# A graph network with expert layers: signals for four groups together, and selections made eight groups ahead, in three of its four edge sums

## The reference

```python
def _gcn_layer(x, W, b, src, dst, norm, n_nodes):      # layers 0 and 1
    xt = x @ W
    msg = xt[src] * norm[:, None]
    agg = jax.ops.segment_sum(msg, dst, num_segments=n_nodes)
    return jax.nn.relu(agg + b)

def gcn_conv(h, W, b):                                 # layers 2 and 3
    m = (h @ W)[src] * norm[:, None]
    return jax.ops.segment_sum(m, dst, num_segments=n) + b

x = x + _L0_gnn_ref(_layernorm(x), ...)                # edge sums 0 and 1
x = x + _L0_ffn_ref(_layernorm(x)[None], ...)[0]       # two of eight experts for all nodes
x = x + _L1_gnn_ref(_layernorm(x), ...)                # edge sums 2 and 3
x = x + _L1_ffn_ref(_layernorm(x)[None], ...)[0]       # one of eight experts for each node
```

## Time and profile before

| what | value |
|---|---|
| device time, median of 3 | 6543.07 us (6539.58 to 6545.11) |
| the profiled execution | 6551.94 us, span 6550.3 us |
| busy, share of the span | PE 55%, PE's weight loads 41%, DVE 39%, ACT 14%, POOL 54% |
| layer 0, layer 1 | gathers from 233 and 1701 us on |
| layer 2, layer 3 | gathers from 3420 and 4687 us on |
| gathers | 3328, 946 ns each |
| mean granted clock of TensorE | 0.755 |

### The profile page before, as it was taken

The page is one execution under the profiler, slowest core; times in us unless marked ns, Lnnn a source line. Parts: engine busy times, 40 slices in busy tenths (PEclk is TensorE's granted clock), DMA queues, the critical chain, the costliest instruction groups (busy, mean ns, idle before and its releaser), DMA issues.

```text
span 6550.3 us, 48736 instructions
## 1 busy us (share of the span) xinstructions
PE 3613.2 (55%) x14645; PEld 2676.9 (41%) x14646; DVE 2556.9 (39%) x6904; ACT 934.1 (14%) x2571; POOL 3523.5 (54%) x3846
## 2 busy tenths in 40 slices
PE   7475444444644434358984444444644444457899
PEld 6353333333433323245663332333433333346566
DVE  7366545555343334335442322222322222233244
ACT  6303222222200000012220000000200000004221
POOL 7705666666466666640006666666366666652232
PEclk9788766767876766678996676676767777676999
DMA  2403333333333333320013333333333333323321
GB/s 82 130 3 107 92 90 93 91 92 88 101 92 91 92 92 92 89 63 20 17 34 91 92 94 91 92 92 92 92 88 92 95 89 92 92 83 124 91 94 47
DMA packets 281242, 552.98 MB, mean 84 GB/s; under 512 B 86322, under 2 KB 167075, under 8 KB 280977
## 3 DMA queue, kind: packets, MB, share of 16 engines
q0 software_dynamic: 168496, 457.67, 24.5%
q1 hardware_dynamic: 106214, 85.77, 4.2%
q10 hardware_dynamic: 6268, 6.40, 0.3%
HBM read 490.90 MB, written 61.69 MB: 84 GB/s over the span
## 4 chain that ended last, share of the span: by engine, by line
another core or an unknown queue 37%; PE 29%; DVE 16%; issue 10%; ACT 3%; POOL 2%; DVEq 2%; DMA 1%; SPq 0%; ACTq 0%; POOLq 0%
PE PSA L740 10%; DVE ACC L1475 5%; PE PSA L983 3%; PE PSA L973 3%; PE PSA L863 3%; PE PSA L875 3%; DVE XIN L1448 2%; POOL WORK L565 2%; DVE XIN L1622 1%; DVE XT L1448 1%; PE PSA L694 1%; PE PSA L700 1%; PE PSA L786 1%; ACT ACC L1019 1%
## 5 line engine op out<-in xcount | busy, mean ns | idle before, releaser
L565 POOL DMA_INDIRECT WORK<-tab,SRC x3284 | 3106.6, 946 | 2424.0 <-issue 992.6
L740 PE MATMUL PSA<-WORK,XIN 128*128 128x256 f32 x3984 | 1300.9, 491 | 1543.2 <-DVE XIN L1448 507.0
L1475 DVE TENSOR_TENSOR ACC<-ACC,PSA 64x256 f32 x1664 | 696.2, 418 | 2982.2 <-remote 2361.6
L740 PEld LDWEIGHTS PSA<-WORK,XIN 128*128 128x128 f32 x3984 | 959.7, 249 | 1875.3 <-issue 1522.7
L740 PE MATMUL PSA<-WORK,XT 128*128 128x256 f32 x2584 | 845.8, 490 | 1058.2 <-DVE XT L1448 342.5
L740 PEld LDWEIGHTS PSA<-WORK,XT 128*128 128x128 f32 x2584 | 621.2, 249 | 1271.3 <-issue 1055.6
L1059 ACT ACTIVATE WORK<-PSA 128x256 f32<-128x256 f32 x147 | 54.0, 376 | 2462.3 <-PE PSA L773 2461.9
L1448 DVE TENSOR_TENSOR XIN<-PSA,DST 128x512 f32<-128x512 f32 x378 | 256.3, 679 | 1.9 <-DVE PSA L1459 1.7
L983 PE MATMUL PSA<-ACC,WORK 128*128 128x256 f32 (+1 forms) x1024 | 223.2, 380 | 6.1 <-ACT WORK L1249 6.1
L973 PE MATMUL PSA<-WORK,ACC 128*128 128x489 f32 (+1 forms) x512 | 214.3, 579 | 5.1 <-ACT WORK L1239 5.1
L983 PEld LDWEIGHTS PSA<-ACC,WORK 128*128 128x128 f32 (+1 forms) x1024 | 189.0, 185 | 43.0 <-ACT WORK L1249 12.4
(11 more groups left out here) (282 smaller groups left out, 3478.2 us busy)
## 6 DMA issues: line engine op xcount, KB each, us to landing
WORK<-tab,SRC POOLq DMA_INDIRECT x3284
ACC<-in_L_ffn_w SPq DMA_DIRECT2D x16, 1024.0 KB
tab<-WORK SPq DMA_DIRECT2D x98, 128.0 KB, 1.7
tab<-ACC SPq DMA_DIRECT2D x98, 128.0 KB, 1.8
slots_x<-FILL SPq DMA_DIRECT2D x4, 2080.0 KB
ACC<-slots_x SPq DMA_DIRECT2D x8, 910.0 KB
before_y<-X SPq DMA_DIRECT2D x7, 896.0 KB
X<-in_x ACTq DMA_DIRECT2D x1, 6144.0 KB
```

What stands on the lines that cost most here:

```text
L565: po.indirect_dma_start(out=rows[:, 0:width], out_offset=None, in_=tab[:, :], in_offset=bass.IndirectOffsetOnAxis(ap=SRC[:, c:c + 1].bitca ...
L740: last = pe.matmul(PS[h][:, 0:D], chosen[:, j * P:(j + 1) * P], rows[:, 0:D], start=(j == 0), stop=(j == Q - 1))
L1475: return ve.tensor_tensor(rows, rows, PS[h][half, 0:D], ALU.add)
```

## The change

In layers 1 to 3 the groups are put in batches (`starts`): 51 of four groups and, at the end, one of two and two of one. PE raises `s_p` only with the last matmul of a batch, by the number of groups in it, and DVE waits only ahead of a batch's first add, for the whole batch. The sums of a batch go to one pair of banks, two groups in a bank (`sums_of`); batches take the pairs `PS[0]`, `PS[1]` and `PS[2]`, `PS[3]` in turn, and PE waits at `s_free`, ahead of the first group that it writes to a bank, until the groups that stood there two batches before are added (`last_in_bank`). Adds still raise `s_free` for each group. Selections are made `FAR` = 8 groups ahead, in eight buffers of their own, `SELF`, in `WORK` behind the ring of rows. Layer 0 keeps its order; its calls only name the bank in another way.

```diff
+FAR = 8
...
+        SELF = [WORK[:, RS_ * Q * ROW1 + k * Q * P:RS_ * Q * ROW1 + (k + 1) * Q * P] for k in range(FAR)]
...
+        starts = list(range(0, NGR - 4, 4)) + [NGR - 4, NGR - 2, NGR - 1, NGR]
+
+        def batch_of(layer, g):
+
+            if not layer:
+                return g, g + 1
+            k = max(k for k in range(len(starts)) if starts[k] <= g)
+            return starts[k], starts[k + 1]
+
+        def sums_of(layer, g):
+
+            if not layer:
+                return PS[g % 4][:, 0:D]
+            k = max(k for k in range(len(starts)) if starts[k] <= g)
+            pos = g - starts[k]
+            return PS[k % 2 * 2 + pos // 2][:, pos % 2 * D:(pos % 2 + 1) * D]
+
+        def last_in_bank(layer, g):
+
+            k = max(k for k in range(len(starts)) if starts[k] <= g)
+            pos = g - starts[k]
+            if not layer or pos % 2 or k < 2:
+                return None
+            return min(starts[k - 2] + pos + 1, starts[k - 1] - 1)
+
+        def chosen_of(layer, g):
+            return SELF[g % FAR] if layer else SEL[g % NS]
...
-                    product(SEL[g % NS], rows_of(layer, g), g % 4).then_inc(s_p, 1)
+                    if last_in_bank(layer, g) is not None:
+                        pe.wait_ge(s_free, 4 + NGR * layer + last_in_bank(layer, g) + 1)
+                    last = product(chosen_of(layer, g), rows_of(layer, g), sums_of(layer, g))
+                    first, end = batch_of(layer, g)
+                    if g == end - 1:
+                        last.then_inc(s_p, end - first)
...
                         for j in range(Q):
                             c = Q * g + j
-                            last = ve.tensor_scalar(SEL[g % NS][:, j * P:(j + 1) * P], PLACES, DST[:, c:c + 1],
+                            last = ve.tensor_scalar(SELF[g % FAR][:, j * P:(j + 1) * P], PLACES, DST[:, c:c + 1],
                                                     NRM[:, c:c + 1], ALU.is_equal, ALU.mult)
                         last.then_inc(s_sel, 1)
                     else:
-                        place(SEL[g % NS], edges(DST, g)).then_inc(s_sel, 1)
+                        place(SELF[g % FAR], edges(DST, g)).then_inc(s_sel, 1)
...
-                for g in range(AHEAD):
+                for g in range(FAR):
                     load_spots(g)
                     choose(g)
 
                 for g in range(NGR):
                     spot = spots_of(g)
-                    ve.wait_ge(s_p, NGR * layer + g + 1)
-                    add_sums(g % 4, spot).then_inc(s_free, 1)
-                    if g + AHEAD < NGR:
-                        load_spots(g + AHEAD)
-                        choose(g + AHEAD)
+                    first, end = batch_of(layer, g)
+                    if g == first:
+                        ve.wait_ge(s_p, NGR * layer + end)
+                    add_sums(sums_of(layer, g), spot).then_inc(s_free, 1)
+                    if g + FAR < NGR:
+                        load_spots(g + FAR)
+                        choose(g + FAR)
                     between(g)
                     ve.wait_ge(s_free, 4 + NGR * layer + g + 1)
```

More of the change, by code:

```diff
@@ L736, in _, with product @@
             pe.reg_mov(turn, 16 * Q)
-            def product(chosen, tiles, h):
+            def product(chosen, tiles, into):
                 for j, rows in enumerate(tiles):
-                    last = pe.matmul(PS[h][:, 0:D], chosen[:, j * P:(j + 1) * P], rows[:, 0:D],
+                    last = pe.matmul(into, chosen[:, j * P:(j + 1) * P], rows[:, 0:D],
                                      start=(j == 0), stop=(j == Q - 1))
@@ L762, in sum_edges @@
                                 pe.wait_ge(s_mx, pe.snap(more))
-                                product(SELX, ROWS[0:Q], 0).then_inc(s_pe, 1)
+                                product(SELX, ROWS[0:Q], PS[0][:, 0:D]).then_inc(s_pe, 1)
                                 pe.reg_add(more, more, 1)
@@ L1469, in sum_of, with add_half, add_sums @@
                 return ve.tensor_reduce(into, by_window(weighted), AX.X, ALU.add)
-            def add_half(h, upper, spot):
+            def add_half(sums, upper, spot):
                 half = slice(P // 2, P) if upper else slice(0, P // 2)
                 rows = ACC[half, bass.ds(spot, D)]
-                return ve.tensor_tensor(rows, rows, PS[h][half, 0:D], ALU.add)
-            def add_sums(h, spot):
-                add_half(h, True, spot[0])
-                return add_half(h, False, spot[1])
+                return ve.tensor_tensor(rows, rows, sums[half, :], ALU.add)
+            def add_sums(sums, spot):
+                add_half(sums, True, spot[0])
+                return add_half(sums, False, spot[1])
             def a_tile(v):
@@ L1519, in wide_groups @@
                                 ve.reg_add(zu, zu, D)
-                                chained(add_half(0, True, a_tile(ve.snap(zl))))
-                                chained(add_half(0, False, a_tile(ve.snap(zu))))
+                                chained(add_half(PS[0][:, 0:D], True, a_tile(ve.snap(zl))))
+                                chained(add_half(PS[0][:, 0:D], False, a_tile(ve.snap(zu))))
                                 ve.reg_mov(zx_next, zl)
@@ L1607, in sum_weighted @@
                     ve.wait_ge(s_p, g + 1)
-                    step(add_sums(g % 4, spot))
+                    step(add_sums(sums_of(0, g), spot))
                     settle()
```

## The result

The changed kernel takes 6555.67 us (20 runs, 6543.0 to 6562.34) against 6543.76 us for the kernel before, run beside it (20 runs, 6538.71 to 6554.74): a ratio of 1.0016, with an interval of 1.0009 to 1.0022. The forecast was 6160 us with a range of 6080 to 6510; the time lies outside it, on the side of no gain. The profiled execution took 6557.08 us (span 6555.4).

The account below looks back on a forecast made before the run. POOL's gathers, stopped by late PE signals, were taken as the bound: 6551.94 us less 457.1 (438.4 surplus, 18.7 tail) gives 6094.8; 75 us of remaining pauses makes 6170, with the 0.14% about 6160, range 6080 to 6510.

Parts of the forecast that it names:

- What bounds the kernel now: Layers 1 to 3: POOL's gathers wait for DVE's adds, which wait for PE's queued signals; surplus 438.4 us.
- What remains: Layers 1 to 3: signals 20 us apart mostly drain; 5 pauses a layer of 5 us stay, 75 us.
- Signals: PE to DVE: 54 signals a layer in place of 208, 20.0 us apart in place of 5.0.
- Selections eight ahead: DVE's selections: PE's 419.3 us of waits in layer 1 go, but by itself this moves nothing POOL waits for.
- What the batch costs: Batch's first sum told 15 us later; free if signals are less than 13.3 us late, before 28.3.
- New waits: PE's waits for adds before reusing a bank pair, and about 100 wait instructions: zero cost.
- The tail: Layer ends, last gather to last add: 6.7 us in place of 15.3, 13.4 and 10.1, saving 18.7 us.
- The floor: Layers 1 to 3 if POOL never stops, 1038.8 us of gathers each: 457.1 us off, 6094.8 us.
- B: Rival: lateness grows with gathers since POOL last stood; 26 stops a layer, 6504 up to 6552 us; chance 0.13.
- A: Rival: lateness grows with signal count, only POOL's pause clears it; 13 pauses a layer, 6290 us; chance 0.27.
- C: Rival: signals pass only in POOL's pause, one pause per batch; 51 a layer, 6878 us; chance 0.08.
- D: Rival: the matmul itself is late, not its signal, so the change does nothing; 6552 us; chance 0.07.

Follow-up runs that it names:

- e10: Changed kernel, but each layer 1 batch signal reaches VectorE by way of ScalarE, which makes 40 small activations first: 7060.93 us (ratio 1.0791).
- e15: Kernel before, with one 128x1 memset on POOL ahead of each gather of layers 1 to 3: 6562.37 us (ratio 1.0021).
- e1: Changed kernel with PE signalling each group again, selections still eight ahead, on a chip with prompt signals: 5818.98 us (kernel before 5818.02).
- e5: Changed kernel without any edit, on a chip with prompt signals: 5813.62 us (kernel before 5818.42).
- e17: Changed kernel with PE making only one of a group's four products in layers 1 to 3: 6455.66 us (ratio 0.9859 to the kernel before).

## Why the prediction was wrong

First what the runs have in common. From a layer's first gather to its last one's end, layers 2 and 3, the time is 1185 and 1185 us before, 1189 and 1189 changed, 1182 and 1182 with a ring of twelve, 1187 and 1183 with half the bytes, 1190 and 1188 with half the rows, 1177 and 1186 with pauses; it is 1043 and 1042 where signals are prompt. Per gather 1.43 against 1.25 us.

- **What bounds the kernel now.** Held as far as it went: POOL waits for adds, adds for signals, and the sums of the three surpluses are right. The step that failed is its reading, "what stands in line is a signal for every group", and with it **What remains**, "that a signal's lateness comes from the signals just before it, and that 20 us let most of it drain". With 54 signals a layer in place of 208 the second batch was told 22 us late, the third promptly in POOL's restart, and the stops summed to what the gathers before them called for (8.6 us after 60 us of gathering, in one stop or in two). So what was done here to signals did not shorten the sum of stops. The 75 us of pauses came out at 445.
- **Signals** and **Selections eight ahead**: held. PE's 419 us of waits for selections went and moved nothing that POOL waits for, as said; the changed kernel on the other chips shows both at no cost.
- **What the batch costs**: the first batch ended at 25.40 us by the trace and its signal came at 25.91; 25.4 was forecast. The slack of 13.3 us is not contradicted, but never decided anything: in `e10` a signal's lateness was not an amount to be set against it, as it started to count in POOL's stop.
- **New waits**: zero held on the other chips. Here PE was held by something else, the 2.80 us spacing.
- **The tail**: 15 us gained for 18.7. The last add is over 7.8 us after the last gather; 6.7 was taken.
- **The floor** of 1038.8 us a layer was taken from the spacing of two gathers. On these chips it is not the floor. The trace of before had the sign: three layers with 33, 40 and 37 stops, with 2.2 us of DVE's work a group in one and 1.53 in two, and surpluses of 148.7, 144.9 and 144.7 us. Sums so equal over stops so different point to a rate.
- **The rivals.** B came near in time (up to 6552, which lay outside the range) and had the pattern, a stop every eight groups in layer 1 (mostly twelve in layers 2 and 3) and lateness that grows with the gathers since POOL last stood, and a chance of 0.13. But a fixed price for each stop is refuted by the ring of twelve: the stops changed in number and length, and their sum did not. I set B aside because an add 14 us after a restart waited in rows 6; that signal was 5.4 us late, more than 0.15 us for each of the 11 gathers since the restart, and this stays unexplained. A is out (stops every eight or twelve groups, not sixteen), C is out (26 stops or fewer, not 51). D's time, 6552, is as near as B's. As a matmul that ends late it is argued against, not excluded: on the other chips all signals follow their matmuls at once, but there nothing is held back. Something close to it is true, which I argued away by PE's restart within 0.15 us of a selection: with the selections ahead, PE's matmuls themselves are held. The Trainium skill's figure that D cited, 26.3 ns from one increment to the next ("TensorE: Matmul & The Clock Gate", section "The cost: per-tile semaphore tail"), is not seen in a trace of this case either: where several of PE's signals come through together in one stop of the kernel before, they are 0.09 us apart.

**What is shown and what is not.** Shown: on three chips with late signals the time of layers 1 to 3 hardly depends on signals, selections, the ring, bytes, row width or rows per gather; POOL's stops sum to what its gathering since the last ones calls for; with a quarter of PE's products four in ten of POOL's gathers in layers 2 and 3 are 1.40 us apart; and PE, and now and then ACT and DVE, are spaced by multiples of 0.70 us too. Argued only: that one and the same backlog makes all of this. Open: what it is, why two chips have none of it, why PE's work has a part in it (31 to 50 us a layer), and why layer 0 stands 358 us. Every gather of every run signalled its landing 16 times; that count was never varied. A run with gathers truly spaced at 1.40 us, the test that `e15` was meant to be, is missing too. And one rival was not tested at all: for every execution on record span and clock were recorded, so none is known that ran without the profiler, and it is on the slower chips that the trace lacks most of its semaphore events. Whether writing these records is itself what lags can't be told from these runs.

## What to carry to other kernels

Before you price stops one by one, compare their sums over stages whose inner work differs: if the sums agree to a few per cent while number and length don't, look for a pace, and test it by moving the stops (a pause put in, a longer ring) before restructuring what seems to release them. A late signal is only worth removing if something else doesn't then become late by the same amount; here the one form with the same sums that was faster than before was a 2.2 us pause of POOL after every four groups, by 0.23%, 16 us. And where a program's bound is a handshake between engines, time both kernels on more than one chip: here the same two took 5818 and 5814 us on one chip and 6544 and 6556 on another.

## What the runs showed of the hardware

- The same program took 5818 us on two chips and 6543 to 6546 on the others, 12% more, at the same length of a gather (946 to 949 ns) and of a selection. Some 695 of the 725 us lie where POOL gathers.
- On the slower ones the trace has few of the landing events: 2468 of the 13312 in layer 2 of the kernel before, with 90 in the first 10 us and 7 to 36 in each 10 us after. On the quicker ones all 13312 are there (`e1`, `e5`). So events are merged or lost in the trace on the chips where PE is held back, which may be the same cause. Some of PE's signals are missing from the trace as well (186 to 193 of 208 are there in a layer of before).
- On the slower chips PE is held at one matmul record of 0.58 us each 2.80 us, up to 182 times a layer, with "issue" as the only reason given; other spacings met there are 2.10, 1.40 and 0.70 us.
- PE's signals are late there by up to 45 us with the ring of twelve (its second batch ended at 44.7 us and was told at 89.75). DVE and ACT mostly keep their pace, but not always: DVE's pairs of adds in `e17`, ACT's activations in `e10` and POOL's gathers in `e17` fall into the same 1.40 and 0.70 us.
